# Two PSUM evictions of a delta-rule attention move from VectorE to ScalarE, and a weight load takes another wait (hybrid layer, 8 cores)

## The reference

```python
x = x + _L0_attn_a_ref(_layernorm(x), W_write, W_read, W_beta, decay)
x = x + _L0_ffn_ref(_layernorm(x), w_gate, w_up, w_down)      # 2816 wide
x = x + _L0_attn_b_ref(_layernorm(x), Wqkv, Wo)               # softmax, 16 heads of 64
x = x + _L0_ffn_ref(_layernorm(x), w_gate, w_up, w_down)
```

```python
v_new = v_i - kcd_i @ S
o_i = k_i * de @ S + attn @ v_new
S_new = chunk_total_decay * S + jnp.einsum('bhcd,bhce->bhde', k_i * dw, v_new)
```

## Time and profile before

| | us |
|---|---|
| median of 2 runs | 6578.74 (6555.77 to 6601.72) |
| profiled execution | 6626.67 |
| its span on the slowest core, core 4 | 6624.8 |
| spans of the other cores | 6518.7 to 6613.2 |
| first attention's tiles, core 4 | about 330 to 2268 |
| first feed-forward part | 2291 to 3830 |
| second attention | 3830 to 5200 |
| second feed-forward part | 5200 to 6624 |

### The profile page before, as it was taken

How to read it: one execution, slowest core, us unless ns; L and a number is a source line. 1 busy time by engine, 2 the same in 40 slices (tenths; PEclk the granted TensorE clock), 3 DMA queues, 4 the chain that set the end, 5 groups by cost and what they waited for, 6 DMA issues and landing times.

```text
span 6624.8 us, 47879 instructions; the slowest of 8 cores (6518.7 to 6624.8 us)
## 1 busy us (share of the span) xinstructions
PE 2860.9 (43%) x14150; PEld 1411.4 (21%) x14344; DVE 4021.8 (61%) x4321; ACT 1027.7 (16%) x1231; POOL 198.8 (3%) x296
## 2 busy tenths in 40 slices
PE   0133333323333252526253367767776434444453
PEld 0022222222222121212121122222332111212121
DVE  0477777777677539384857455446544475665835
ACT  0211111111111200000000116600662000000000
POOL 0010100001010000000000000000000000000000
PEclk9955555555555576868676689977787667666666
DMA  7011111111111121313131100010001112121223
GB/s 125 20 35 36 38 35 39 36 34 38 34 36 35 30 62 46 94 35 94 46 94 46 37 16 1 1 35 16 1 1 42 51 46 79 55 75 39 76 62 116
DMA packets 278304, 303.92 MB, mean 46 GB/s; under 512 B 98202, under 2 KB 213658, under 8 KB 277794
## 3 DMA queue, kind: packets, MB, share of 16 engines
q1 hardware_dynamic: 258242, 236.33, 12.2%
q0 software_dynamic: 19808, 64.53, 4.2%
HBM read 266.15 MB, written 38.27 MB: 46 GB/s over the span
## 4 chain that ended last, share of the span: by engine, by line
DVE 51%; PE 27%; DMA 7%; issue 7%; ACT 5%; SPq 2%; DVEq 1%; another core or an unknown queue 0%; ACTq 0%; PEldq 0%; POOL 0%; POOLq 0%; PEld 0%
PE PS L1072 6%; PE PS L1068 5%; DVE bigB L1691 3%; DMA bigB<-wuT_scr 3%; ACT med L1668 2%; PE PS L322 2%; PE PS L1624 2%; DVE bigA L1172 2%; DVE bigA L1187 2%; DVE bigA L1189 2%; DVE bigA L1176 2%; DVE qcol L1122 2%; PE PS L1558 2%; PE PS L1745 2%; DVE bigB L816 2%
## 5 line engine op out<-in xcount | busy, mean ns | idle before, releaser
L1668 ACT ACTIVATE med<-PS 128x1024 bf16<-128x1024 f32 x512 | 524.3, 1024 | 765.8 <-PE PS L1639 599.4
L1087 DVE TENSOR_TENSOR bigC<-PS,bigB 128x512 bf16<-128x512 f32 (+1 forms) x192 | 124.3, 647 | 813.8 <-ACT bigB L1080 810.8
L322 PE MATMUL PS<-c_eye,bigA 128*128 128x128 bf16 (+1 forms) x1120 | 124.3, 286 | 778.3 <-DVE bigA L1203 331.5
L1080 ACT ACTIVATE bigB<-PS 128x512 bf16<-128x512 f32 (+1 forms) x192 | 107.8, 562 | 2223.2 <-PE PS L1072 2223.2
L1639 PE MATMUL PS<-med 128*128 128x512 bf16 x976 | 327.4, 426 | 171.4 <-ACT med L1668 99.8
L1068 PE MATMUL PS<-bigB,med 128*128 128x512 bf16 (+1 forms) x744 | 289.0, 400 | 207.2 <-DMA bigB<-wuT_scr 207.2
L1072 PE MATMUL PS<-med 128*128 128x512 bf16 x768 | 318.7, 415 | 21.2 <-DVE xres L557 18.0
L322 PE MATMUL PS<-c_eye,bigB 128*128 128x128 bf16 (+1 forms) x608 | 60.5, 274 | 593.5 <-DVE bigB L1203 590.9
L1022 PE MATMUL PS<-bigA,bigB 128*128 128x512 bf16 x920 | 265.6, 418 | 113.2 <-DMA bigA<-wdT_scr 75.6
L1068 PE MATMUL PS<-med 128*128 128x512 bf16 x736 | 305.1, 415 | 1.0 <-DVE med L329 1.0
L1072 PE MATMUL PS<-bigB,med 128*128 128x512 bf16 (+1 forms) x768 | 298.3, 400 | 2.7 <-issue 1.5
(11 more groups left out here) (208 smaller groups left out, 6234.3 us busy)
## 6 DMA issues: line engine op xcount, KB each, us to landing
bigA<-wdT_scr SPq DMA_DIRECT2D x236, 256.0 KB, 2.9
bigB<-wdT_scr SPq DMA_DIRECT2D x116, 256.0 KB, 2.9
med<-wgT_scr SPq DMA_DIRECT2D x24, 1024.0 KB, 10.5
med<-wuT_scr SPq DMA_DIRECT2D x24, 1024.0 KB, 11.7
bigB<-wgT_scr SPq DMA_DIRECT2D x16, 1024.0 KB, 5.7
bigB<-wuT_scr SPq DMA_DIRECT2D x16, 1024.0 KB, 8.4
bigC<-wg POOLq DMA_DIRECT2D x44, 256.0 KB, 3.1
bigC<-wu POOLq DMA_DIRECT2D x44, 256.0 KB, 3.2
```

What stands on the lines that cost most here:

```text
L322: self.t(lambda t, sap=sap, i=i: t.transpose(self.bankb(bank)[0:prow, i * 128:(i + 1) * 128], sap, self.CST["eye128"][:]), inc=(i == n - 1))
L1668: self.s(lambda s, sb=sb, ptb=ptb: s.activation(out=ptb, in_=self.PS[:, sb * 512:(sb + 2) * 512], func=AF.Exp, scale=0.125), inc=True)
```

## The change

Three edits. The copies of bank 2 to `vnew8` and of bank 4 to `SST` in each half of the state update go from DVE to ACT (64 instructions in all). The load of Wo waits for PE's newest instruction at the time of its emission; before, it waited for `_tok_wo`, which was taken at the beginning of `attn_b` and after each half of the product.

```diff
-                self.read_bank(2, "vector")
-                self.v(lambda v, half=half: v.tensor_copy(
+                self.read_bank(2, "scalar")
+                self.s(lambda s_, half=half: s_.copy(
                     out=vnew8[:, half * 512:(half + 1) * 512], in_=self.bankf(2)),
                     inc=True)
-                self.bank_read_done(2, "vector")
-                tok_vn = self.em.tok("vector")
+                self.bank_read_done(2, "scalar")
+                tok_vn = self.em.tok("scalar")
...
-                self.read_bank(4, "vector")
-                self.v(lambda v, half=half: v.tensor_copy(
+                self.read_bank(4, "scalar")
+                self.s(lambda s_, half=half: s_.copy(
                     out=SST[:, half * 512:(half + 1) * 512], in_=self.bankf(4)),
                     inc=True)
-                self.bank_read_done(4, "vector")
+                self.bank_read_done(4, "scalar")
...
-        self._tok_wo = self.em.tok("tensor")
         self.v(lambda v: v.memset(MED2[64:128, 0:4096], 0.0), inc=True)
...
-                    wait=[self.tok_cast["wo16"], self._tok_wo])
+                    wait=[self.tok_cast["wo16"], self.em.tok("tensor")])
...
-                self._tok_wo = self.em.tok("tensor")
```

## The result

The changed kernel takes 0.9825 of the time before, with a 95% interval from 0.978 to 0.987: some 115 us less of 6578. The forecast was 105.8 us less. In some executions of either kernel one die or both run at a lower clock and take longer, so the ratio compares fast executions alone, the medians of all (57 us apart) understate the gain, and the rows of after are those of core 5 (span 6411.0 us), on the die that was not slowed in the profiled execution.

What follows compares the result with a forecast made beforehand. DVE's own queue plus its few waits was taken to bound the first attention. Gains of 125.2 us less 19.4 lost made 105.8 us, from 6578.74 to 6472.9; range 6420 to 6560, the forecast's own 6440 to 6510.

Steps and rivals of the forecast that it cites:

- The bound: First attention: time is DVE's own queue plus its few waits, DVE occupied for 1546 of 1878 us.
- 64 x 0.79 = 50.6 us: State update: 64 copies (L859, L900) leave DVE's queue, each 0.69 us plus its gap, gaining 50.6 us.
- 71.0 + 3.6 us of waits: State update: DVE's waits for matmuls L888 (71.0 us) and L852 (3.6 us) go with the copies.
- The chain over ACT: State update to transposes, before L329: 9.3 us over PE and ACT, hidden under 11.9 us of DVE background instructions.
- Rival B: Idle time only moves: DVE waits before L329 instead of for L888; gain 34.8 us, 6544; chance 0.11.
- The last tile: First attention's end: some 3 us of DVE wait against part of the waits before L816 filled; both put at zero.
- The tile: First attention: each tile about 7.6 us shorter, named as a sign that the forecast is right.
- The tail: Head of the feed-forward stage: DVE waits for the last background task's store, 12.4 us lost, exposed once.
- Wo: Load of Wo's first half now waits for PE's L1701 matmuls: 7.0 us lost for both passes.
- C: First attention: PE, ACT and DVE chain paces the tile, copies save nothing; 44.9 us slower, 6624; chance 0.05.
- E: Background work is paced by its transfers: no gain comes and 19.4 us are lost, 6598; chance 0.04.
- D: First attention: granted clock rises where DVE waits for PE (L703, L917); 53 us more gained, 6420; chance 0.08.

Runs made afterwards that it cites:

- e5: Changed kernel with 64 DVE instructions put back where the copies stood; first feed-forward L542 starts at 2218.3 us, against 2168.2 in the changed kernel.
- e4: Changed kernel with only the SST copy (L900) on ACT, L859 back on DVE; first feed-forward L542 at 2192.1 us, against 2168.2.
- e3: Changed kernel with only the vnew8 copy (L859) on ACT, L900 back on DVE; first feed-forward L542 at 2193.3 us, against 2168.2.
- e10: Kernel before the change, with all background work moved after the first attention; 15 tiles take 1026.3 us (core 0).
- e11: Changed kernel, with all background work moved after the first attention; 15 tiles take 1033.2 us (core 0).
- e6: Changed kernel with DVE's two waits for PE (L852, L888) put back in each half, no instruction; first feed-forward L542 at 2174.3 us, against 2168.2.
- e7: Changed kernel with each of the L859 and L900 copies done twice on ACT; first feed-forward L542 at 2171.0 us, against 2168.2.
- e8: Changed kernel with 7 instead of 6 background steps after each half; first feed-forward L542 at 2156.1 us, against 2168.2.
- e2: Changed kernel with both copies back on DVE, only Wo's load wait changed; first feed-forward L542 at 2287.1 us, against 2288.5 before the change.
- e9: Changed kernel with background steps moved ahead of DVE's waits, Wo's load as before; 0.9671 of the time before, first feed-forward L542 at 2055.7 us.

## Why the prediction was right

- **The bound.** DVE's queue sets the tile: shown by e5 (50.1 us for 50.6 us of work), by e4 with e3 (PE's wait before L869 costs nothing), and by e10 with e11.
- **64 x 0.79 = 50.6 us** was right, gap and all.
- **71.0 + 3.6 us of waits** went in full. The reason given, that nothing left on DVE waits for L888, was true but not the whole cause: e3 and e6 have that wait and pay some 7 us for it, in one tile. The round trip is the cause, and either move alone ends it.
- **The chain over ACT** lies under DVE's steps with 4.4 to 9.3 us to spare in the first 15 tiles (core 5), where 2 to 3 were worked out. Counted as in the forecast, from the first matmul (L847) to the end of the transposes, it takes 7.2 to 8.4 us in 14 of them and 9.4 in one, in which all of PE's matmuls took 0.31 us and not 0.22; the forecast had 9.3. In that one the cover is 14.7 us (975.7 to 990.4) and not 11.9. Rival B falls with e7, for a chain up to 3 us longer.
- **The last tile** was put at nothing on both sides. It has one wait of 3.9 us before L329, and 1.6 us less for L807.
- **What was left out.** The tiles and the tail were to bring the mark 112.8 us forward, and it came 120.3. On core 5, where it came 122.9, DVE's waits show terms that the sum didn't have: 7.6 us less for L807, 2.5 for L917 and 4.0 for transfers, against 3.8 more for L322. With the 1.5 us less that Wo cost, this is why the forecast of 105.8 came out some 9 us short.
- **The tile** was to be about 7.6 us shorter, and is 10.8 shorter. The sign left out that the four steps pushed back also leave the tile, 3.4 us by the forecast's 0.85 a step; they come again behind the last tile.
- **The tail**, 12.4 us, measured 11.7 us of DVE's wait. The 12.1 us of e8 agree by chance, since other terms stand in them.
- **Wo**, 7.0 us, measured 5.4 (core 0) and 5.6 (core 5) by e2 beside before: the load in flight covered what was expected, and each wait is 5.6 us instead of 5.9.
- **Rivals.** C asked for a tile of unchanged length, and E for late loads. The tile is shorter, and DVE's waits in the tiles put down to a load's or transpose's DMA are 1 to 10 us after, where they were 9 to 12 before (cores 0, 4, 5 and 7). No load fell behind. For D, the granted clock of the stage is 0.57 (core 5) against 0.56, and the waits for L703 and L917 are nearly unchanged.

With 0.84 for a change within 2% and a ratio of 0.9825 whose interval ends at 0.978, the forecast and the measurement say the same, that the gain lies near that line.

## What to carry to other kernels

Ask whose queue the time is before pricing a move. That PE waits 193 us for a copy does not make these 193 us the gain; the gain is what comes off the queue of the engine that never has room. Count an instruction taken off such an engine with its gap, and its waits only as far as no background work is queued ahead of them. Where filler work shares an engine with waits, put the filler ahead of the wait and let the wait find its work done: that gave 100 us here (e9 against e8), nearly as much again as the whole change.

## What was not expected

The copies moved to the engine with room made an ordinary tile 0.2 us longer where DVE wasn't full (e10, e11), though a copy is 0.59 us on ACT and 0.69 on DVE.

The gains of the two moves don't add: 95.2 and 96.4 us alone, 120.3 together. Each would have looked like four fifths of the change. The sum of the two is 71.3 us too large, about the 71.0 us of waits for L888 that either of them ends.

The output's transposes now also wait for the last copy of `SST`, since the token they wait for is ACT's newest (13.3 us in 11 waits of L322 for ACT's L900 on core 5). It cost nothing under DVE's cover.
